# A vision tower's last stage on one core: from two buffers with everything on the Vector engine to three buffers shared by ScalarE and the Vector engine

## The reference, cut to what matters

```python
def _layernorm(x, axis=-1, eps=1e-05):
    m = jnp.mean(x, axis=axis, keepdims=True)
    v = jnp.var(x, axis=axis, keepdims=True)
    return (x - m) / jnp.sqrt(v + eps)
...
for e in range(E):
    mid = jax.nn.relu(jnp.einsum('bsd,fd->bsf', x, W1[e]) + b1[e])
    ye = jnp.einsum('bsf,df->bsd', mid, W2[e]) + b2[e]
    out = out + w[..., e:e + 1] * ye
return out
...
h = _layernorm(h + _L0_ffn_ref(h, ...), axis=-1)
```

## Time and profile before

| | us |
|---|---|
| median of 3 runs | 5095.28 |
| lowest and highest run | 5089.06, 5112.28 |
| the profiled execution, its own time | 5082.8 |
| its span, first to last instruction | 5081.0 |
| busy in the span: TensorE | 4568.4 (90%) |
| Vector engine | 3744.7 (74%) |
| ScalarE | 3051.0 (60%) |
| GpSimd | 310.8 (6%) |

### The profile page before, as it was taken

The page is one execution under the profiler, slowest core; times in us unless marked ns, Lnnn a source line. Parts: engine busy times, 40 slices in busy tenths (PEclk is TensorE's granted clock), DMA queues, the critical chain, the costliest instruction groups (busy, mean ns, idle before and its releaser), DMA issues. The chain is left out here.

```text
span 5081.0 us, 191812 instructions
## 1 busy us (share of the span) xinstructions
PE 4568.4 (90%) x84561; PEld 3640.2 (72%) x84562; DVE 3744.7 (74%) x8549; ACT 3051.0 (60%) x4474; POOL 310.8 (6%) x349
## 2 busy tenths in 40 slices
PE   5999999885999999999999999999999278599990
PEld 4777777642788888888888888888888144377770
DVE  8999999743577777777777777777777644355557
ACT  4777777633566666666666666666664234377771
POOL 0000000000000000000000000000000014433330
PEclk9999999986999999999999999999999576699995
DMA  1000000032000000000000000000000222322214
GB/s 63 33 35 27 27 27 27 29 98 66 14 16 17 22 16 16 22 17 16 16 23 16 16 21 17 16 16 23 16 12 9 92 89 97 112 69 67 71 60 152
DMA packets 164003, 203.02 MB, mean 40 GB/s; under 512 B 66736, under 2 KB 141744, under 8 KB 160752
## 3 DMA queue, kind: packets, MB, share of 16 engines
q1 hardware_dynamic: 149680, 159.86, 10.5%
q0 software_dynamic: 13632, 32.66, 1.8%
HBM read 123.64 MB, written 68.81 MB: 38 GB/s over the span
## 5 line engine op out<-in xcount | busy, mean ns | idle before, releaser
L653 PE MATMUL y_ps<-k_sb,x_sb 128*12 128x256 f16 x58368 | 1683.4, 273 | 13.3 <-DVE x_sb L890 13.0
L653 PEld LDWEIGHTS y_ps<-k_sb,x_sb 128*12 128x12 bf16 x58368 | 1425.6, 88 | 186.9 <-issue 24.4
L772 ACT ACTIVATE y_sb<-y_ps 128x256 f32<-128x256 f32 x912 | 348.3, 382 | 841.8 <-PE y_ps L653 841.8
L781 ACT ACTIVATE k_new<-cos,k_bias 128x512 f32<-128x512 f32 x768 | 520.9, 683 | 171.2 <-PE cos L680 171.2
L663 PEld LDWEIGHTS turned_x<-rows_in,y_sb 128*128 128x128 f32 x3648 | 477.7, 191 | 118.3 <-issue 71.6
L921 DVE CUSTOM_DVE_ANT_0 plan<-plan,u_rows,v_last 128x512 f32<-128x512 f32 x768 | 535.2, 744 | 4.3 <-issue 0.3
L663 PE MATMUL turned_x<-rows_in,y_sb 128*128 128x16 f32 x3648 | 526.6, 258 | 8.4 <-ACT y_sb L772 8.2
L256 PE MATMUL acc<-w_hl,feat_h 128*128 128x384 f16 x2688 | 454.6, 327 | 87.5 <-ACT feat_h L241 87.5
L795 ACT ACTIVATE plan<-plan,p_bias,p_scale 128x1024 f32<-128x1024 f32 x384 | 464.2, 1238 | 9.7 <-DVE p_scale L932 9.7
L909 DVE TENSOR_TENSOR plan<-k_sb 128x1024 f32<-128x1024 f16 x384 | 459.3, 1217 | 0.0
L936 DVE TENSOR_TENSOR k_sb<-k_new,k_sb 128x2048 f16<-128x2048 f32 x192 | 436.1, 2272 | 30.4 <-ACT k_sb L789 30.4
(11 more groups left out here) (256 smaller groups left out, 7199.3 us busy)
## 6 DMA issues: line engine op xcount, KB each, us to landing
x_in_sb<-expert_rows SPq DMA_DIRECT2D x39, 528.0 KB, 3.7
xt<-in_x_dram SPq DMA_DIRECT2D x16, 1280.0 KB, 5.9
q_left<-q_parts SPq DMA_DIRECT2D x192, 64.0 KB, 3.0
q_right<-q_parts SPq DMA_DIRECT2D x192, 64.0 KB, 3.0
y<-expert_results SPq DMA_DIRECT2D x32, 384.0 KB, 3.7
v_parts<-v_sb SPq DMA_DIRECT2D x16, 408.0 KB, 2.4
v_in_sb<-v_parts SPq DMA_DIRECT2D x48, 136.0 KB, 3.5
h_tokens<-h_sb SPq DMA_DIRECT2D x16, 384.0 KB, 2.5
```

Source lines behind the costliest of these rows:

```text
L653: last = nc.tensor.matmul(y[a][32 * c:32 * c + XW, :, :], high[:, j, XW * h:XW * (h + 1)], k_sb[s][:, h, :, at:at + P], start=(h == 0 and ...
L772: nc.scalar.activation(y_sb[a][:, :, :], y[a][:, :, :], ACT.Copy).then_inc(rows_read[a], 1)
L781: nc.scalar.activation(k_new[h % 2][:, c, :], cos[:, c % 2, :], ACT.Exp, bias=k_bias[:, 0:1], scale=1.0 / (REG * Q_SCALE ** 2), accum_out= ...
```

## The change

`combine` is rewritten. Its buffers become rings of three (`DEEP`), `second`, `shift` and `inv_std` among them; `share` and its copy are gone, since all code is unrolled and the shares are read in place from `share_all`. The work is divided anew:

- ScalarE: `weigh(i)` multiplies the second results by their shares into `second` (four Copy with a scale pointer), `deviation(i)` is the square root, `normalise(i)` writes the outputs as inv_std * acc + shift (four Identity with scale and bias pointers). Its order is weigh(0), and then for each i: weigh(i+1), deviation(i), normalise(i-1).
- Vector engine: `add(i)` adds the first results to `x_all` (four instructions); `scales(i)` takes the reciprocal and shift = -mean * inv_std; `statistics(i)` adds `second` in one instruction of 128x768 and takes the statistics. Its order is, for each i: add(i), scales(i-1), statistics(i).
- SP: load(i) now waits, from image 3 on, until image i-3 has been added and weighed; it loads the second results first. Its order is, for each i: load(i), store(i-2). The stores wait for `out_ready`, which ScalarE now signals.

```diff
@@ -1788,94 +1788,124 @@
             counters.append(ctx.enter_context(nc.semaphore(name)))
             return counters[-1]
...
+        DEEP = 3
+        ring = lambda name, shape, dt: [sb(f"{name}{r}", shape, dt) for r in range(DEEP)]
+        share_all, x_all = keep["share_all"], keep["x_all"]
+        y = ring("y6", [P, PICKS, DIM], F32)
+        second = ring("second6", [P, TB, DIM], F32)
+        acc = ring("acc6", [P, TB, DIM], F32)
+        stats, mean_var = sb("stats6", [P, TB, 6], F32), ring("mean_var6", [P, TB, 2], F32)
+        std, inv_std, shift = ring("std6", [P, TB], F32), ring("inv_std6", [P, TB], F32), ring("shift6", [P, TB], F32)
+        out_sb = ring("out_sb", [P, TB, DIM], F32)
+        idle = sb("idle6", [P, 3], F32)
+        second_ready, added, summed, stat_steps, var_ready = (
+            sem("second_ready"), sem("added"), sem("summed6"), sem("stat_steps"), sem("var_ready"))
+        std_ready, inv_ready, shift_ready, out_ready = sem("std_ready6"), sem("inv_ready"), sem("shift_ready"), sem("out_ready")
+        y_in, out_done = [sem(f"y_in6{r}") for r in range(DEEP)], [sem(f"out_done{r}") for r in range(DEEP)]
         block = ctx.enter_context(nc.Block())
...
         @block.sync
         def _(sp):
             for counter in counters:
                 sp.sem_inc(counter, START)
...
+            def load(i):
+                if i >= DEEP:
+                    sp.wait_ge(added, START + i - DEEP + 1)
+                    sp.wait_ge(second_ready, START + i - DEEP + 1)
+                for choice in (1, 0):
+                    src = results[i * TOKENS + choice * ALL_TOKENS:(i + 1) * TOKENS + choice * ALL_TOKENS, :]
+                    sp.dma_start(y[i % DEEP][:, choice * TB:(choice + 1) * TB, :],
+                                 src.rearrange("(b p) d -> p b d", p=P)).then_inc(y_in[i % DEEP], 16)
+            def store(i):
                 sp.wait_ge(out_ready, START + i + 1)
...
-            staged(sp, load, nothing, store)
...
+                sp.dma_start(out[i:i + 1, :, :, :].rearrange("a p b d -> (a p) b d"), out_sb[i % DEEP][:, :, :]).then_inc(out_done[i % DEEP], 16)
+            for i in range(IMAGES + DEEP - 1):
+                if i < IMAGES:
+                    load(i)
+                if i >= DEEP - 1:
+                    store(i - DEEP + 1)
+            for r in range(DEEP):
+                sp.wait_ge(out_done[r], START + 16 * len(range(r, IMAGES, DEEP)))
         @block.scalar
         def _(act):
...
+            def weigh(i):
+                act.wait_ge(y_in[i % DEEP], START + (i // DEEP + 1) * 32)
+                if i >= DEEP:
+                    act.wait_ge(summed, START + i - DEEP + 1)
+                for b in range(TB):
+                    last = nc.scalar.activation(second[i % DEEP][:, b, :], y[i % DEEP][:, TB + b, :], ACT.Copy,
+                                                scale=share_all[:, i, TB + b:TB + b + 1])
+                last.then_inc(second_ready, 1)
+            def deviation(i):
                 act.wait_ge(var_ready, START + i + 1)
...
-            staged(act, deviation)
+                nc.scalar.activation(std[i % DEEP][:, :], mean_var[i % DEEP][:, :, 1], ACT.Sqrt, bias=keep["eps"][:, 0:1]).then_inc(std_ready, 1)
+            def normalise(i):
+                act.wait_ge(shift_ready, START + i + 1)
+                if i >= DEEP:
+                    act.wait_ge(out_done[i % DEEP], START + i // DEEP * 16)
+                for b in range(TB):
+                    last = nc.scalar.activation(out_sb[i % DEEP][:, b, :], acc[i % DEEP][:, b, :], ACT.Identity,
+                                                bias=shift[i % DEEP][:, b:b + 1], scale=inv_std[i % DEEP][:, b:b + 1])
+                last.then_inc(out_ready, 1)
+            weigh(0)
+            for i in range(IMAGES + 1):
+                if i + 1 < IMAGES:
+                    weigh(i + 1)
+                if i < IMAGES:
+                    deviation(i)
+                if i >= 1:
+                    normalise(i - 1)
         @block.vector
         def _(dve):
...
+            def add(i):
+                r = i % DEEP
+                dve.wait_ge(y_in[r], START + (i // DEEP + 1) * 32)
+                if i >= DEEP:
+                    dve.wait_ge(out_ready, START + i - DEEP + 1)
+                nc.vector.memset(idle[:, 0:1], 0.0)
                 for b in range(TB):
...
+                    last = nc.vector.scalar_tensor_tensor(acc[r][:, b, :], y[r][:, b, :], share_all[:, i, b:b + 1], x_all[:, i * TB + b, :],
+                                                          ALU.mult, ALU.add)
+                last.then_inc(added, 1)
+            def statistics(i):
+                r = i % DEEP
+                dve.wait_ge(added, START + i + 1)
+                dve.wait_ge(second_ready, START + i + 1)
+                nc.vector.tensor_tensor(acc[r][:, :, :], acc[r][:, :, :], second[r][:, :, :], ALU.add).then_inc(summed, 1)
+                dve.wait_ge(summed, START + i + 1)
+                nc.vector.memset(idle[:, 1:2], 0.0)
                 for b in range(TB):
...
+                    nc.vector.bn_stats(stats[:, b, :], acc[r][:, b, :]).then_inc(stat_steps, 1)
+                dve.wait_ge(stat_steps, START + i * TB + TB)
+                nc.vector.memset(idle[:, 2:3], 0.0)
                 for b in range(TB):
...
+                    last = nc.vector.bn_aggr(mean_var[r][:, b, :], stats[:, b, :])
                 last.then_inc(var_ready, 1)
+            def scales(i):
+                r = i % DEEP
                 dve.wait_ge(std_ready, START + i + 1)
...
-            staged(dve, take, add)
+                nc.vector.reciprocal(inv_std[r][:, :], std[r][:, :]).then_inc(inv_ready, 1)
+                dve.wait_ge(inv_ready, START + i + 1)
+                nc.vector.scalar_tensor_tensor(shift[r][:, :], mean_var[r][:, :, 0], -1.0, inv_std[r][:, :], ALU.mult,
+                                               ALU.mult).then_inc(shift_ready, 1)
+            for i in range(IMAGES + 1):
+                if i < IMAGES:
+                    add(i)
+                if i >= 1:
+                    scales(i - 1)
+                if i < IMAGES:
+                    statistics(i)
```

More of the change, by code:

```diff
@@ L1789, in sem @@
             return counters[-1]
[L1791 to L1802, removed]
-        block = ctx.enter_context(nc.Block())
[L1805 to L1810, removed]
+        DEEP = 3
[12 more added lines that the diff above has]
+        y_in, out_done = [sem(f"y_in6{r}") for r in range(DEEP)], [sem(f"out_done{r}") for r in range(DEEP)]
+        block = ctx.enter_context(nc.Block())
         @block.sync
@@ L1815, in _ @@
                 sp.sem_inc(counter, START)
[L1817 to L1824, removed]
-                sp.wait_ge(out_ready, START + i + 1)
-                sp.dma_start(out[bass.ds(i, 1), :, :, :].rearrange("a p b d -> (a p) b d"), out_sb[a][:, :, :]).then_inc(out_done[a], 16)
@@ L1828, in _ @@
-            staged(sp, load, nothing, store)
-            for a in range(2):
-                sp.wait_ge(out_done[a], START + 16 * IMAGES // 2)
+            def load(i):
[6 more added lines that the diff above has]
+                                 src.rearrange("(b p) d -> p b d", p=P)).then_inc(y_in[i % DEEP], 16)
@@ L1832, in _ @@
         @block.scalar
         def _(act):
-            def deviation(i, a):
-                act.wait_ge(var_ready, START + i + 1)
-                nc.scalar.activation(std[:, :], mean_var[:, :, 1], ACT.Sqrt, bias=keep["eps"][:, 0:1]).then_inc(std_ready, 1)
-            staged(act, deviation)
+            def weigh(i):
[6 more added lines that the diff above has]
+                last.then_inc(second_ready, 1)
@@ L1840, in _ @@
+            weigh(0)
[6 more added lines that the diff above has]
+                    normalise(i - 1)
         @block.vector
         def _(dve):
[L1842 to L1850, removed]
-                for b in range(TB):
[L1852 to L1855, removed]
+            def add(i):
[4 more added lines that the diff above has]
+                nc.vector.memset(idle[:, 0:1], 0.0)
+                for b in range(TB):
+                    last = nc.vector.scalar_tensor_tensor(acc[r][:, b, :], y[r][:, b, :], share_all[:, i, b:b + 1], x_all[:, i * TB + b, :],
+                                                          ALU.mult, ALU.add)
+                last.then_inc(added, 1)
@@ L1856, in add @@
+            def statistics(i):
[5 more added lines that the diff above has]
+                nc.vector.memset(idle[:, 1:2], 0.0)
                 for b in range(TB):
-                    nc.vector.scalar_tensor_tensor(acc[a][:, b, :], y[a][:, TB + b, :], share[a][:, TB + b:TB + b + 1], acc[a][:, b, :],
-                                                   ALU.mult, ALU.add).then_inc(added, 1)
@@ L1859, in add @@
-                dve.wait_ge(added, START + i * PICKS + PICKS)
-                nc.vector.memset(idle[:, :], 0.0)
```

(13 more changed lines are left out.)

## The result

| | before | after |
|---|---|---|
| median of 20 runs, us | 5093.37 | 5117.86 |
| lowest and highest | 5084.43, 5112.28 | 5104.13, 5145.13 |
| span of the profiled execution | 5081.0 | 5103.7 |
| images in the last stage, first addition to last output | 105.21 | 133.21 |

The changed kernel is slower: ratio 1.0051, 95% interval 1.0037 to 1.0065, that is +26 us (19 to 33) where +29.7 was forecast; the two medians themselves are 24.5 apart. It lies at the edge of the 0.5% that I had named as what can be told apart, and the interval does not hold 1.

A forecast was written before the change was run, and what follows sets the result against it. Before, the Vector engine's chain bound the last stage; after, a circle through SP, loads and ScalarE: 0.03 + 0.39 + 4.3 + 0.6 + 0.05 + 3.73 = 9.1 us per image. With start and end, 5095.28 + 29.7 = 5125.0 us, range 5106 to 5138.

The forecast's parts named there:

- The loop: Last stage: load(i+1) stands behind store(i-2), which waits for ScalarE's newest output; ScalarE waits next for that load.
- The turn: Time per image in the last stage's steady part, a sum of serial steps: 9.1 us against 6.63 before.
- Store to load: On SP, from the store's issue to the first load's issue: 0.39 us per image.
- The pair alone: An image's two loads, until both have landed, without a store's effect: 4.3 us, bounds 3.9 to 4.6.
- The store's contention: Extra landing time of the two loads from the store ahead in their queue: 0.6 us, bounds 0 to 1.2.
- ScalarE 3.73: ScalarE's weighings, square root and outputs per image, in series with the loads: 3.73 us, bounds 3.6 to 4.1.
- The page against the rows: Landing of store and two loads from the store's issue: 4.7 us by the skill page, 5.3 by trace rows, which were kept.
- The start: Last stage's first images: first loads land at 4973.2 us, outputs of image 0 end at 4984.3.
- Rival A: Last stage: same circle of waits but the store costs loads nothing; 8.3 us per image, +19 us, 5114 us; chance 0.31.
- Rival B: Last stage: three buffers hide the loads, Vector engine sets 4.6 us per image; -28.7 us, 5067 us; chance 0.05.
- The DVE's 4.6 us an image: Vector engine work per image in the changed last stage: 4.6 us, against 6.63 before.
- Rival C: ScalarE reloads tables between Sqrt and Identity, twice 1.28 us per image: +63 us, 5158 us; chance 0.04.

The follow-up runs named there:

- Experiment 1: Changed kernel with SP issuing load(i) before store(i-3) instead of store(i-2): turn 4.47 us, stretch 78.1 us, ratio 0.9935 to the kernel before.
- experiment 5: Changed kernel with SP issuing load(i) before store(i-3), but load(i) made to wait needlessly for out_ready(i-3): turn 8.51 us, stretch 130.1 us.
- 4: Changed kernel with four more weighings per image on ScalarE, into a spare buffer, ahead of the real ones: turn 10.26 us, stretch 153.9 us.
- 3: Changed kernel with one more 128x768 addition per image on the Vector engine: turn 8.85 us, stretch 136.0 us.
- 2: Changed kernel with four buffers instead of three, SP's order kept: turn 8.92 us, stretch 136.5 us.
- experiment 9: Changed kernel with SP issuing load(i), then store(i-4) instead of store(i-2): turn 4.08 us, stretch 73.3 us, ratio 0.9926 to the kernel before.
- experiment 10: Changed kernel with SP only loading and ScalarE issuing each store on its own queue after its outputs: turn 4.08 us, stretch 74.5 us.

## Why the prediction was right

The direction, the mechanism and the size were right: 5125.0 against 5117.86, +29.7 against +26. Some of the closeness is luck: four terms of the turn were off, measured less forecast, by -0.29, +0.23, -0.20 and +0.06 us, which leaves -0.20, and a start that was 1.5 us too short made up for part of that.

- **The loop**: as forecast. Experiment 1 opens it, 5 closes it again with one wait, 4 shows ScalarE in it, 3 and 2 show that the DVE and the buffers are not. The forecast that removed DVE work is worth nothing there holds: 15.3 us of added work disappear.
- **The turn**, 9.1 forecast, 8.90 measured. Store issue 0.03: 0.03. Store to load 0.39: 0.45. The pair alone 4.3 with waking 0.05: 4.58. The store's contention 0.6: 0.40. ScalarE 3.73: 3.44. The mis-sized term is ScalarE's, which fell below its own bounds of 3.6 to 4.1. Its instructions were each 12 or 13 ns shorter, and the overlap of about 0.09 holds across a satisfied wait too (5005.02 for the deviation, while the weighing that began at 5003.62 ran until 5005.11). My 3.73 is 1.55 + 0.30 + 1.91 = 3.76 less only 0.03, where the overlaps at the two edges take off 0.18.
- **The page against the rows**: the estimate from the Trainium skill, "DMA: Bandwidth & Descriptors", section "Anatomy of one DMA — SWDGE (gpsimd) path", was 4.7 us for store and pair. The trace gives 0.45 + 4.98 = 5.43 from the store's issue, so the measurement does not agree with what I carried over from it (the page gives its fit for another issuing path and for a single transfer); the rows' 5.3 was nearer.
- **The start** was off by +1.5. I let the first stored image come 11.1 us after the first addition (4984.3 - 4973.2); it came 12.6 after. The second pair landed 4.5 us behind the first, not 2.4, which the first statistics hid all but 0.4 of, and the table load, which I had put before the data or behind the DVE's statistics, stands after weigh(1), on the path: the DVE waits 1.73 us for the first deviation.

```profile
4972.33 1.49 ACT L1840 ACTIVATE second<-y,share_all 128x192 f32<-128x192 f32 x4 [3.05 <-DMA y<-expert_results]
...
4973.84 1.28 ACT L1846 ACT_TABLE_LOAD   x1
4975.14 0.30 ACT L1846 ACTIVATE std<-mean_var,eps 128x4 f32<-128x4 f32 x1
```

  Why the second pair took 4.5 us was not tried; in other runs with the same first loads it was 3.4 to 4.5. In the sum the start and the shorter turns (12 x 0.2 = 2.4) and an end 0.7 shorter make 2.4 + 0.7 - 1.5 = 1.6, which is 137.5 - 135.9, forecast and measured stretch. The unrolled code, priced at nothing, shows no cost in the middle: ScalarE's outputs have no idle time before them (0.0 in their group above).
- **Rival A** (a cheap loop): the turn of 8.90 is just above the 8.8 that separated it. The measured +26 on a limit of 25.5, with an interval of 19 to 33, can't separate the two cases. The trace does: the sign named for A was less than 4.7 us from the store's issue to the weighing, and it is 5.43.
- **Rival B** (buffers hide the loads) did not come true, but its arithmetic was the right one for another order: -28.7 us forecast, and the first experiment ran at 0.9935, -33. The DVE's 4.6 us an image was too high: 4.08 in experiment 9, where the first addition, the reciprocal and the sum each start some 0.08 us before what stands ahead of them has ended (the reciprocal at 5018.48, the additions run until 5018.56), and the statistics take 1.48 us until the next addition instead of 1.58. It is the term of the forecast that was worst, and it had no effect because it was off the path.
- **Rival C** (tables): one table load, ahead of the first Sqrt, served Sqrt, Copy and Identity for the 16 images (the first eight Copies ran before it). By the Trainium skill, "ScalarE: Activation LUTs", section "Table sets: the hidden batching unit", copy and identity are in every set; the trace agrees.

## What to carry to other kernels

A wait in an in-order queue also holds back everything behind it. Before adding buffers or moving work between engines, write down for each queue which engine's output it waits for and what stands behind; if the same engine waits for that next, the turn is the sum of the whole circle, here with four buffers as with three. The order load, then an older store, cost nothing here and was worth 58 us of stretch.

## What the runs showed of the hardware that was not expected

A store of 384 KB costs a pair of loads the same whether it is issued 0.45 us ahead of the first (4.98 us from issue to weighing) or right behind the second (5.04), against 4.58 without one; I had expected one behind to cost less (4.4 to 4.7). Over the turns of each trace these times run from 4.82 to 5.12, from 4.82 to 5.50 and from 4.43 to 4.76 us.

The store itself is slower behind loads. Time to landing, the last number of a row, first of experiment 1 (issues from 4998 to 5050 us), where the store is issued 0.45 us ahead of the pair, and then of experiment 10 (the same window), where it stands in ScalarE's queue:

```profile
y<-expert_results SPq DMA_DIRECT2D x22, 384.0 KB, 4.3
out_dram<-out_sb SPq DMA_DIRECT2D x12, 384.0 KB, 2.8
```

```profile
y<-expert_results SPq DMA_DIRECT2D x22, 384.0 KB, 5.0
out_dram<-out_sb ACTq DMA_DIRECT2D x12, 384.0 KB, 5.5
```

A store took 5.5 us instead of 2.8, yet the turn of experiment 10 was the 4.08 of experiment 9. It need not be the second queue: in experiment 10 the store is issued some 0.75 us behind the first load of a pair (5015.12 against 5014.37). In experiment 5 it stands in SP's queue, 0.96 us behind the first load, and took 4.9 us (issues from 5012 to 5100 us):

```profile
out_dram<-out_sb SPq DMA_DIRECT2D x10, 384.0 KB, 4.9
```

So most of the difference goes with the place behind the loads; what the second queue adds was not tried apart from it.
